# Swin block, attention loop: four value-placing DMAs of each unit issued by ScalarE instead of SyncE

## What is computed

```
xn  = layernorm(x) * g1 + b1;  rolled by (-3, -3), cut into 1024 windows of 49 tokens
q, k, v = split(xn @ qkv_w + qkv_b)                      per window and head
attn = softmax(q * scale @ k^T + position_bias + mask)   49 x 49 per head
x1  = x + unroll((attn @ v) @ proj_w + proj_b)
out = x1 + gelu(layernorm(x1) @ fc1_w + fc1_b) @ fc2_w + fc2_b
```

## Time and profile before

| | us |
|---|---|
| median of 3 runs | 1219.42 (1214.75 to 1219.89) |
| the profiled execution | 1203.71 |
| its span, first to last instruction | 1201.9 |
| attention phase in it, about | 865 |
| MLP phase in it, about | 297 |

### The profile page before, as it was taken

How to read it: one execution, slowest core, us unless ns; L and a number is a source line. 1 busy time by engine, 2 the same in 40 slices (tenths; PEclk the granted TensorE clock), 3 DMA queues, 4 the chain that set the end, 5 groups by cost and what they waited for, 6 DMA issues and landing times. The chain is left out here.

```text
span 1201.9 us, 47188 instructions
## 1 busy us (share of the span) xinstructions
PE 990.5 (82%) x16452; PEld 798.1 (66%) x16452; DVE 1055.9 (88%) x2454; ACT 928.1 (77%) x2242; POOL 812.9 (68%) x907
## 2 busy tenths in 40 slices
PE   1588888989888898888888988898882888878877
PEld 0377777777777777777777777777771555555555
DVE  6799899989999999999999999999964888999996
ACT  0378787777877777777787778788773889999997
POOL 6267676666766666666666666677654767888883
PEclk9999999999999999999999999999995889999999
DMA  1122222222222222222222222222210011111111
GB/s 49 38 63 74 63 56 63 67 64 56 60 66 62 61 57 67 65 61 55 60 70 63 56 60 71 64 60 72 54 43 0 29 32 35 35 35 40 35 35 48
DMA packets 87016, 64.50 MB, mean 54 GB/s; under 512 B 53699, under 2 KB 86756, under 8 KB 86966
## 3 DMA queue, kind: packets, MB, share of 16 engines
q1 hardware_dynamic: 86966, 63.83, 20.1%
HBM read 10.48 MB, written 9.63 MB: 17 GB/s over the span
## 5 line engine op out<-in xcount | busy, mean ns | idle before, releaser
L376 POOL TENSOR_TENSOR pl<-p,ph 113x294 f16<-113x294 f32 x512 | 393.2, 777 | 163.8 <-ACT p L435 159.2
L221 POOL TENSOR_TENSOR rstd<-var,mhalf 112x7 f32<-112x7 f32 x128 | 192.6, 1505 | 134.3 <-DVE var L216 134.3
L741 DVE TENSOR_REDUCE rowmax<-banks 113x12 f32<-113x588 f32 x256 | 192.3, 751 | 55.4 <-PE banks L564 52.9
L433 ACT ACTIVATE ph<-banks 113x294 f16<-113x294 f32 x512 | 216.1, 422 | 25.4 <-PE banks L580 21.6
L580 PE MATMUL banks<-Qh,KAg 128*128 128x147 f16 x2048 | 223.7, 232 | 0.0
L435 ACT ACTIVATE p<-banks 113x294 f32<-113x294 f32 x512 | 213.9, 418 | 0.0
L580 PEld LDWEIGHTS banks<-Qh,KAg 128*128 128x128 f16 x2048 | 171.8, 99 | 34.1
L596 PE MATMUL banks<-Vb,ph 113*128 113x36 f16 x3072 | 184.0, 181 | 1.1 <-POOL pl L376 1.1
L596 PE MATMUL banks<-Vb,pl 113*128 113x36 f16 x1536 | 169.4, 180 | 0.0
L596 PEld LDWEIGHTS banks<-Vb,ph 113*128 113x128 f16 x3072 | 161.4, 97 | 11.0 <-POOL pl L376 1.4
L408 ACT ACTIVATE KM<-banks,lorow 128x392 f16<-128x392 f32 x128 | 75.2, 587 | 103.7 <-PE banks L498 103.6
(11 more groups left out here) (120 smaller groups left out, 2891.1 us busy)
## 6 DMA issues: line engine op xcount, KB each, us to landing
Qh<-QAB SPq DMA_DIRECT2D x192, 98.0 KB, 2.2
Vb<-Vn SPq DMA_DIRECT2D x256, 54.0 KB, 2.0
xres<-in_x SPq DMA_DIRECT2D x64, 147.0 KB, 2.2
KAh<-KA SPq DMA_DIRECT2D x192, 49.0 KB, 1.9
out_y<-ybuf SPq DMA_DIRECT2D x64, 147.0 KB, 2.0
Qh<-mT SPq DMA_DIRECT2D x128, 4.6 KB, 2.2
w<-in_weights SPq DMA_DIRECT2D x1, 278.9 KB
mask<-in_maskt SPq DMA_DIRECT2D x1, 257.2 KB
```

The source lines that it names most:

```text
L221: nc.gpsimd.tensor_tensor(rstd[:, :], var[:, :], mhalf[:, :], ALU.pow).then_inc(s_pow, 1)
L376: nc.gpsimd.tensor_tensor(pl[p % 4][:, :, :, 0:N].rearrange("p a w n -> p w a n"), p32[p % 4][:, :, :, :], ph[p % 4][:, :, :, 0:N].rearran ...
L433: nc.scalar.activation(ph[p % 4][:, :, :, 0:N].rearrange("p a w n -> p w a n"), src, ACT.Exp, scale=1.0 / SB)
L741: nc.vector.tensor_reduce(rowmax[:, 2 * p:2 * p + 4, :].rearrange("p (k w) a -> p k (w a)", k=2), sc[0:AP_, :, 0:2 * COLS].rearrange("p k ...
```

## The change

The four DMAs of line 351 leave SP's `step` together with their two waits, and are put into ACT's `step` between the copy to `xT` and `exp(t-1, 3)`. Shapes, buffers and semaphores stay as they are. SP's wait for `s_vlow`, which only stood in the last step, becomes a wait in every step on ACT.

```diff
@@ SyncE's step @@
                     if not exists(t + 1):
                         sp.wait_ge(s_qlow, 2 * done(t))
-                        sp.wait_ge(s_vlow, done(t))
                     wait(sp, s_st, PAIRS * done(t - 2))
                     for hp in range(HP):
                         sp.dma_start(Qh[par][hp:ROWS:HP, :, hp, :, :], QAB[par][hp:ROWS:HP, :, :, :]).then_inc(s_tb[par], 16)
-                    wait(sp, s_pv, PAIRS * done(t - 2))
-                    for w in range(2):
-                        for g in range(G):
-                            sp.dma_start(Vb[par][g * GP:(g + 1) * GP, :, w, g, :],
-                                         Vn[par][w * GP:(w + 1) * GP, :, g, :, :].rearrange("p l a d -> p l (a d)"))\
-                              .then_inc(s_vb[par], 16)
@@ ScalarE's step, behind the copy to xT @@
+                if exists(t):
+                    act.wait_ge(s_vlow, done(t))
+                    wait(act, s_pv, PAIRS * done(t - 2))
+                    for w in range(2):
+                        for g in range(G):
+                            act.dma_start(Vb[par][g * GP:(g + 1) * GP, :, w, g, :],
+                                          Vn[par][w * GP:(w + 1) * GP, :, g, :, :].rearrange("p l a d -> p l (a d)"))\
+                               .then_inc(s_vb[par], 16)
                 if exists(t - 1):
                     exp(t - 1, 3)
```

## The result

The changed kernel takes 1264.15 us (median of 4 runs, 1258.25 to 1266.91) against 1217.36 (4 runs) before: the ratio is 1.038, 95% interval 1.033 to 1.043. It is slower by 47 us; 57 were forecast. Its profiled execution has a span of 1260.4 us, 58.5 more than the one before; where the 12 us between these two differences come from is taken up under the clock, at the end.

What follows compares the result with a forecast made beforehand. DVE was taken to set the step, with ACT leading it by 1.2 us at `v_low`. Longer steps (+37) and clock drops (+20) made +57 on 1219.4, so 1277 us; forecast 1245 to 1300, wider range 1229 to 1328.

Steps and rivals of the forecast that it cites:

- The issues on ACT: ACT between `xT` and `exp(t-1, 3)`: four issues take 2.6 us from about `xT`'s start, delaying that `exp` by 2.2 us.
- The rival of a sequencer that runs past `xT`: ACT's issues begin up to 0.8 us earlier, delay 1.4 us, absorbed by its lead: no change, 1219 us; chance 0.10.
- the small loss: Rival: issues of 0.5 us, delay 1.6 to 1.9, +0.2 us a step, no further drops: +12, 1231 us; chance 0.10.
- What the delay reaches: Behind the issues: `v_low` 0.5 us late, DVE's sum of squares 0.7, the step 0.6 us longer.
- The threshold of about 1.5 us: ACT's lead at `v_low`, 1.2 us, plus 0.37 idle time: a delay costs only beyond it.
- SP's relief at nothing: Taking four issues and a wait off SP lets nothing that PE, DVE or ACT waits for issue earlier: worth nothing.
- The collision of the two queues: Heavier rival: ACT's first issue collides with SP's last for `Qh`, delay 2.7 us, about 1325 us; chance 0.23.
- the rival of longer issues: Heavier rival's other form: each ACT issue takes 0.1 us more, step +1.1 us, about 1325 us; chance 0.23.
- The clock: More idle time on PE at line 670 brings about 15 further drops of TensorE's clock at 1.3 us: +20.
- The +57: Whole forecast loss on the profiled execution: 37 for longer steps plus 20 for the clock, 1203.71 to 1261 us.
- the term of 37 us for the steps: Attention phase: about 62 full steps, each 0.6 us longer, +37 us.
- The faster rival: PE's idle stretch splits in two at delay near 1.4 us, the clock's 15 drops are saved: -20, 1199 us; chance 0.04.

Runs made afterwards that it cites:

- e7_no_v_dma: Kernel before with V's four DMAs and the waits for them left out, pv multiplying by ones: 1214.5 us against 1213.6, ratio 1.001.
- e3_late_slot: The change with its four issues and waits moved behind `exp(t-1, 4)`, the end of ACT's step: 1236 us, ratio to before 1.025.
- e4_issues_only: Kernel before, V still on SP, plus four unused 16 KB DMAs with met waits issued by ACT at the change's place: 1266 us, ratio 1.054.
- e1_two: The change with two of the four V issues given back to SP, two left on ACT: 1181 us against 1207 before, ratio 0.984.
- e12_two_again: The kernel of e1_two run again, with more rounds: ratio to before 0.979 (0.971 to 0.986).
- e6_pe_split: Kernel before plus one wait on PE: `t_scores(t-1, 5)` waits until DVE has written QAg of unit t + 1: ratio 0.998.
- e9_pool_wait: Kernel before plus one wait on GpSimd: its subtraction for `exp(t-1, 3)` waits until DVE has written QAg of unit t + 1: ratio 0.980.
- e5_act_stall: Kernel before plus two useless activations (0.92 us together) on ACT between `xT` and `exp(t-1, 3)`, no DMA moved: 1188 us against 1214, ratio 0.981.

## Why the prediction was right, and where not

**The issues on ACT.** Forecast 2.6 us for four, delay 2.2; measured 2.73 and 2.22, of which 0.15 us come from a cause that the sum did not have (the two queues, below). The reading of the sequencer's records held: in the rows shown it gets past an activation once that one's wait is met, not before. The first issue of the change stands 0.06 us behind `xT`'s start. The rival of a sequencer that runs past `xT` falls; so does the small loss.

**What the delay reaches.** By their distance from the start of `xT`, `v_low` is 0.57 us later than in the earlier trace rows (forecast 0.5; 414.31 + 2.2 - 0.37 gives 416.1, not 416.0, so by its own terms 0.6), DVE's sum of squares 0.8 (0.7), the step 0.63 (0.6). 62 steps of 0.63 make 39 us; 37 were forecast. The threshold of about 1.5 us lies where the runs allow it: 0.91 costs nothing, 1.61 is balanced by shorter work on DVE, 2.22 and 2.27 cost.

**SP's relief at nothing.** Right: e7_no_v_dma.

**The collision of the two queues.** Where the rival expected it, it did not come: SP's three issues for `Qh` beside ACT's first one took 1.93 us, as in the earlier trace rows, their median from 107 to 832 us is 610 ns, and ACT's first issue takes 598 ns in the median (597 in e3_late_slot).

```profile
L346 SPq DMA_DIRECT2D Qh<-QAB x159: 597/610/1121, 107.1 to 831.6; - x159
```

But another pair does show a stretch. SP's load of x begins beside ACT's second issue in 47 of the steps, and there that issue takes 783 ns in the median; in e3_late_slot, with no issue of SP beside it, 631. First the change, SP's load and the second issue, then the second issue in e3_late_slot:

```profile
416.28 0.39 SPq L321 DMA_DIRECT2D xres<-in_x  x1
...
L467 ACTq DMA_DIRECT2D Vb<-Vn x1: 777/777/777, 416.3 to 416.3; - x1
```

```profile
L476 ACTq DMA_DIRECT2D Vb<-Vn x1: 642/642/642, 423.2 to 423.2; - x1
```

So the rival of longer issues was right in kind and small in size: 0.15 us a step, by estimate some 9 us of the loss, as the delay is past the threshold. The Trainium skill ("Perfetto Trace Analysis", section "DMA Instruction — HWDGE (DVE, Sync)") describes a lock on one descriptor generator, for the sequencers of DVE and SyncE. Here it is ACT and SyncE; the 0.15 us would fit such a lock, but the first issue overlaps an issue of SP without any stretch, and no run here decides it.

**The clock.** This is the step that failed: "with 1.8 us at line 670 in every step I expect more, about 15 further ones at 1.3 us: +20". PE's idle time did grow, to 1.53 and 0.15 us, but the phase had 12 drops instead of 15, and as much time at the lower level in the second profile. In 48 steps of the loop (from the ninth copy to `xT` to the 57th) there were 15 drops before and 6 after; the other 6 of the change fell into the steps that are written out, where the kernel before had none. The price was too high as well. Behind 10 of the 15 drops before, the next step is the shorter one, 12.40 us instead of 12.85, which gives back a third of the 1.3 us:

```profile
439.96:452.36 12.40, 11.23 (x199) 9.65 (x198) 12.09 (x27) 10.40 (x27) 9.03 (x11) 1.00 0.26 68
```

Those 48 steps took 644.6 us before and 665.3 after. Without drops they would be 628.3 and 657.8, so the drops cost 16 us before and 7 after: the clock gave 9 us back there, and took an estimated 7 (6 drops at 1.2) in the written-out steps. The term was about -2 us, not +20; some 4 us of the phase's 41 are left in the written-out steps.

**How near the sum came.** The +57 lies close to the 58.5 us between the two profiled executions, and that is luck. Of these, 41 are the phase, and 18 the slower clock of the MLP phase, which e4_issues_only and the two profiles of one kernel (e1_two, e12_two_again) show to differ by as much without the change. The timed runs differ by 47 us, 6 to 8 of them outside the phase as the two profiles of the change have it. What was right is the term of 37 us for the steps. (On the scale of the timed runs 1219.4 + 57 is 1276, not 1277.)

**The faster rival.** It was given 0.04 because the delay would be 2.2 us, and that was right for this change. A gain does exist at a smaller delay, 0.9 us: the clock's drops go from 15 to 2, as the rival had it, and QAg is shorter, which it did not have. That the split of PE's idle stretch is what saves the drops is not shown (e6_pe_split, e9_pool_wait). In the change QAg is shorter as well, 427 ns, but DVE only reaches `v_low` the earlier and waits there 0.70 us. So four issues forfeit what two would bring: with two the phase is 21 us shorter than before, with four 41 longer.

**Left open.** What decides where the drops fall. The sum of PE's idle time does not (it is largest in the change, with fewer drops than before), its longest piece does not either (1.53 us in the change, 12 drops; about 1.0 in e9_pool_wait, 3), and a split alone halved them.

## What to carry to other kernels

An issue of a DMA on ACT held its sequencer for about 0.63 us here, at 16 KB as at 54, and 0.78 where an issue of SP began beside it: lay that against the lead that the engine has over whoever waits for its next results, not against the engine's idle share. ACT was busy 77% of the time, and 2.7 us of issues in a step of 12.85 fitted that on paper; the lead was about 1.5 us. And before moving work off a queue, leave it out once: here that showed there was nothing to win. A small delay of an engine off the critical path can be a gain, if it takes that engine's followers off a stretch in which they slow another; a wait on GpSimd did the same here without a DMA on ACT. And two profiled executions can differ by 19 us in a phase that nothing touched: a part of a difference belongs to a change only if other kernels, and a second profile of the same one, do not show it too.

## What was not expected of the hardware

- DVE's float16 operation on 128x784 elements takes 562 ns in the mean beside GpSimd's subtractions and 427 to 437 when GpSimd's subtraction beside it is put off (e1_two, e5_act_stall, e9_pool_wait). One wait on GpSimd made the kernel 2% faster, shorter steps and fewer drops together.
- ACT's sequencer issued a DMA with one activation under way and two not yet begun (e3_late_slot): an issue hides behind all of those, if their waits are met.
- An issue on ACT took 783 ns where SP's load of x began beside it and 631 where nothing did; beside SP's issue for `Qh` it took no longer (598).
- The share of TensorE's time at 1.2 GHz changed with small shifts of order: 15 drops in the phase before, 0 with two added waits, and 0.87 to 1.00 as the mean clock of the last 250 us in an MLP phase whose code was the same, even between two executions of one kernel; in e1_two it was this:

```profile
925.40:1175.40 250.00, 197.11 (x3569) 133.51 (x3567) 220.19 (x525) 237.46 (x534) 199.21 (x170) 1.00 0.12 38
```
